# First attention of a 16-sequence block on one core: gate features stacked into 96 rows, product with values by quarters, tiles closed a pass later

## The chip, the cores and the metric

The kernel runs on one core of one Trainium2 chip. The metric is the device time of one execution, in microseconds (us); lower is better. The engines are PE (TensorE), DVE (VectorE), ACT (ScalarE), POOL (GpSimd) and SP (SyncE, which here only issues DMAs).

## What is computed

X is 16 sequences of 128 tokens of 256 numbers. It goes through an attention over a context with a relational gate, a feed-forward net, a second attention and a mixture of experts. The change lies in the first attention alone:

```python
q = (queries @ Wq.T + bq).reshape(b, nq, H, D_K).transpose(0, 2, 1, 3)      # H = 16, D_K = D_V = 64
...
g = relu(einsum('bnmd,hd->bhnm', emb, Wg) + bg[None, :, None, None])        # emb: sin and cos of 100 * log box differences
a = einsum('bhqd,bhkd->bhqk', q, k) / sqrt(D_K)
mn = softmax(log(clip(g, 1e-06, None)) + a, axis=-1)
out = einsum('bhqk,bhkd->bqhd', mn, v).reshape(b, nq, H * D_V)
return out @ Wo.T + bo
```

emb has, for each pair of tokens (n, m) of a sequence, the sine and cosine of two frequencies of four differences: of the centres in x and y, relative to a size, and of the logarithms of width and height. The kernel computes the softmax numerator as max(g, 1e-6) * exp(a), so the gate is a factor. Width and height differences split into products of terms of n and of m and come from tables; centre differences don't, and are worked out for each pair.

## The kernel before

A tile is one sequence; there are 16, b = 0 to 15. Each engine runs a program of its own, written out by hand, and they meet at semaphores; the order on an engine is the order of the code. The programs are software-pipelined: in one pass (`iteration(b)`) every engine does a different part for tile b-1, b, b+1 and b+2. Products that need accuracy use pairs of fp16 numbers, a high part (a copy, made by ACT) and a low part (the rest, by a subtraction on POOL), and three matmuls for high x high, high x low and low x high.

One pass of the engines, in words, with the line numbers of the profile:

- **PE**: scores of tile b in four groups (lines 1762, 1769), among them the gates of tile b, one for each of four PSUM banks (`gate`: a table product of `Lst`, line 1784, and the feature product, line 1788, of `F16s` with the block-diagonal weights `We16`), row scores for the maximum (1747), project_qk (1719) of tile b+1, then `pv` of tile b-1 (1807: probabilities with values, four quarters f of 4 heads), project_v (1730), turn_o (1821), turn_xn (1696) and project_o (1827) of tile b-1.
- **VectorE**: `norm` (868), row maxima (879) and take_qk (899) in two pairs each, take_pv (888 the reciprocal of the denominators, 891 the division) of tile b-1, the floor of the centre differences ahead of the logarithm (852), take_v (908), turns (857), xn_low (873), `residual` of tile b-1 (914 writes `otmp`, 917 adds it to X), fractions (861, 863), distance (845), and, when the exponentials of tile b are there, `probs` (928: clip, times exponential) and the statistics of the new X (1017).
- **ScalarE**: exponentials (1424), sine (1393) and the high part of the features (1397), high parts of the probabilities (1450), of q and k (1437) and of v (1442), logarithm (1386), take_o (1408).
- **POOL**: low parts of the probabilities (565, four of them), of the features (560), of q and k (551, four), of v (556, two), of the context (521), and two DMAs that turn a half of one expert's weights to fp16 for a later stage (574, 578).
- **SP**: for each tile a load of context (343), of its gate tables (`load_tables`, 396, three transfers of 68 KB, after the gate of two tiles before), the store (368) and load (374) of expert halves; at b = 8 the second half of the gate tables is stored (386, 387). At the end the weights of the feed-forward net (421 to 424), on which `ternary_scale` (961 on, VectorE) waits.

The features stand with one of 128 rows for each of x or y, sine or cosine, two frequencies and 16 tokens n; columns are the 8 blocks of n and the tokens m. The gate's six matmuls of 256 columns (16 heads x 16 tokens n) use all 128 rows.

## Time and profile before

| | |
|---|---|
| median of three runs | 1148.08 us (1142.33 to 1149.12) |
| profiled execution | 1143.62 us |
| its span, first to last instruction | 1141.6 us |
| busy, of the span | PE 949.0 (83%), VectorE 817.9 (72%), ScalarE 684.2 (60%), POOL 710.1 (62%) |
| mean granted clock of TensorE | 0.929 |

The first attention takes the stretch from about 24 to 480 us, its middle tiles that from 100 to 401. Everything behind 480 us is not touched by the change. The rows that follow below are of this one profiled execution, on a scale that begins with its first instruction.

### The profile page before, as it was taken

What the parts mean: (1) busy time and instruction counts of PE and PEld (TensorE: products, weight loads), DVE (VectorE), ACT (ScalarE), POOL (GpSimd) and SP (SyncE); (2) the same over time, 40 slices, a digit from 0 to 9 for tenths busy, and PEclk for the clock granted to TensorE, in tenths of its full rate; (3) what the DMA queues carried; (4) which work ended last, traced back from release to release, by engine and by line L of the source; (5) the groups of instructions that cost most, each with busy time, mean ns of one, the idle gap of its engine ahead of it and who ended that gap; (6) DMA issues with size and microseconds to landing.
All of it is one profiled execution on the core that took longest, in us unless ns stands there. A gap on an engine that the chain in (4) does not pass through costs nothing.

```text
span 1141.6 us, 32938 instructions
## 1 busy us (share of the span) xinstructions
PE 949.0 (83%) x12178; PEld 777.1 (68%) x12178; DVE 817.9 (72%) x1957; ACT 684.2 (60%) x1342; POOL 710.1 (62%) x811
## 2 busy tenths in 40 slices
PE   0448999999999985589876569982899999999995
PEld 0336777777777764455544458861899999999995
DVE  3997888788877876677877689956566666666663
ACT  2457888888888883066543468854354454545452
POOL 2988888875777653035453279965466666666662
PEclk9889999999999997689988789985899999999998
DMA  9277776787767656411000100003553225832251
GB/s 280 76 188 150 135 150 153 157 175 171 146 154 159 137 109 167 143 51 41 1 1 1 40 2 21 21 21 100 165 152 103 33 40 168 268 91 32 32 143 14
DMA packets 52117, 119.65 MB, mean 105 GB/s; under 512 B 7616, under 2 KB 30144, under 8 KB 51632
## 3 DMA queue, kind: packets, MB, share of 16 engines
q0 software_dynamic: 14144, 35.48, 21.6%
q1 hardware_dynamic: 35520, 80.71, 21.1%
q10 hardware_dynamic: 2352, 2.10, 0.6%
q8 instruction: 66, 1.08, 0.4%
q14 instruction: 35, 0.29, 0.1%
HBM read 212.54 MB, written 37.85 MB: 219 GB/s over the span
## 4 chain that ended last, share of the span: by engine, by line
PE 53%; DVE 14%; POOL 11%; ACT 9%; DMA 7%; issue 5%; SPq 0%; ACTq 0%; POOLq 0%; DVEq 0%
PE bank L2168 17%; PE bank L2182 8%; POOL PT L565 6%; PE bank L1827 5%; PE bank L1730 3%; PE bank L1929 3%; DVE nmx L1209 2%; PE bank L1968 2%; PE bank L1807 2%; ACT EX L1424 2%; PE bank L1941 2%; PE bank L1769 2%; ACT L1393 1%; PE bank L1762 1%; DMA gates<-in_g_ffn 1%
## 5 line engine op out<-in xcount | busy, mean ns | idle before, releaser
L1664 ACT ACTIVATE yg<-bank,bms 128x128 f32<-128x128 f32 x312 | 106.9, 363 | 113.2 <-PE bank L2168 103.3
L1327 DVE TENSOR_TENSOR hm<-hf,hm 128x256 f16<-128x256 f32 x156 | 66.7, 427 | 90.8 <-ACT hm L1671 87.0
L1322 DVE SCALAR_TENSOR_TENSOR hf<-bank,bms,yg 128x128 f32<-128x128 f32 x312 | 98.8, 347 | 32.1 <-ACT yg L1664 29.4
L2168 PE MATMUL bank<-xT,wm_even 128*128 128x128 f16 x1920 | 116.2, 221 | 1.9 <-DVE xT L1334 1.0
L709 POOL DMA_INDIRECT out_x<-ys,sidx x39 | 62.7, 1608 | 83.2 <-DVE ys L1341 83.2
L2168 PEld LDWEIGHTS bank<-xT,wm_even 128*128 128x128 f16 x1920 | 111.5, 99 | 3.5 <-DVE xT L1334 1.4
L2168 PE MATMUL bank<-xT,wm_odd 128*128 128x128 f16 x1824 | 109.9, 220 | 2.0 <-DMA wm_odd<-expert_weights 2.0
L2168 PEld LDWEIGHTS bank<-xT,wm_odd 128*128 128x128 f16 x1824 | 105.5, 99 | 3.1 <-issue 2.2
L1671 ACT ACTIVATE hm<-hf 128x256 f16<-128x256 f32 x156 | 64.7, 415 | 63.9 <-DVE hf L1322 62.8
L565 POOL TENSOR_TENSOR PT<-PT 128x512 f16<-128x512 f32 x64 | 72.3, 1157 | 41.7 <-ACT PT L1450 41.6
L551 POOL TENSOR_TENSOR q<-qt,q 128x512 f16<-128x512 f32 x64 | 79.9, 1276 | 1.0 <-ACT q L1437 0.9
L670 POOL TENSOR_TENSOR P<-P 128x512 f16<-128x512 f32 x64 | 72.9, 1171 | 11.5 <-ACT P L1620 11.5
L635 POOL TENSOR_TENSOR h<-h 128x512 f16<-128x512 f32 x32 | 37.3, 1166 | 50.1 <-ACT h L1524 24.5
L702 POOL DMA_INDIRECT xin<-expert_tokens,gidx x39 | 44.5, 1141 | 30.8 <-POOL b2r L724 26.3
L1827 PE MATMUL bank<-WoT,OT 128*128 128x256 f32 x256 | 59.5, 386 | 1.9 <-ACT OT L1408 1.9
L2182 PE MATMUL bank<-wm_even,hm 128*128 128x256 f16 x480 | 57.4, 278 | 2.3 <-DVE hm L1327 2.3
L1437 ACT ACTIVATE q<-qt 128x512 f16<-128x512 f32 x64 | 38.9, 626 | 34.0 <-DVE qt L899 34.0
L1807 PE MATMUL bank<-vv,PT 128*128 128x65 f16 x768 | 33.9, 200 | 28.0 <-POOL PT L565 17.8
L1827 PEld LDWEIGHTS bank<-WoT,OT 128*128 128x128 f32 x256 | 47.3, 190 | 11.7 <-ACT OT L1408 5.9
L578 POOL DMA_DIRECT2D wsp<-in_wcat x16 | 19.6, 1222 | 56.3 <-ACT wsp L1414 56.0
L719 POOL TENSOR_SCALAR gts<-xin,etf 128x1 f32<-128x1 f32 x78 | 53.4, 911 | 0.7 <-DMA xin<-expert_tokens,gidx 0.6
L1788 PE MATMUL bank<-We,F16s 128*128 128x256 f16 x384 | 53.7, 277 | 0.0
(309 smaller groups left out, 2660.2 us busy)
## 6 DMA issues: line engine op xcount, KB each, us to landing
wm_even<-expert_weights SPq DMA_DIRECT2D x60, 1024.0 KB
wm_odd<-expert_weights SPq DMA_DIRECT2D x57, 1024.0 KB
expert_weights<-in_wcat POOLq DMA_DIRECT2D x16, 768.0 KB, 7.8
wsp<-expert_weights SPq DMA_DIRECT2D x16, 768.0 KB, 4.4
wsp<-in_wcat POOLq DMA_DIRECT2D x16, 768.0 KB, 10.6
expert_weights<-wsp SPq DMA_DIRECT2D x16, 768.0 KB, 3.3
Lst<-gate_tables SPq DMA_DIRECT2D x48, 68.0 KB, 5.8
gate_tables<-Lw SPq DMA_DIRECT2D x6, 512.0 KB, 4.6
```

The costliest lines, as they stand in the source:

```text
L551: nc.gpsimd.tensor_tensor(q16[:, par, w, 1, HS * g:HS * g + HS, :], qt[:, r, :, :], hi, ALU.subtract).then_inc(s_ql, 1)
L565: nc.gpsimd.tensor_tensor(PT16[:, 1, HS * g:HS * g + HS, :], PT[:, HS * g:HS * g + HS, :], PT16[:, 0, HS * g:HS * g + HS, :], ALU.subtract ...
L670: nc.gpsimd.tensor_tensor(P116[:, b % 2, 1, HS * g:HS * g + HS, :], P1[:, b % 2, HS * g:HS * g + HS, :], P116[:, b % 2, 0, HS * g:HS * g + ...
L709: nc.gpsimd.indirect_dma_start(out=a["out"], out_offset=bass.IndirectOffsetOnAxis(ap=sidx[:, t:t + 1], axis=0), in_=ys[:, t % 2, :], in_of ...
L1322: v.scalar_tensor_tensor(hf[:, (c // 2) % 2, c % 2, :], bank[c % 4][:, MT:2 * MT], bms[:, par, FC + c:FC + c + 1], yg[:, c % 4, :], ALU.ad ...
L1327: v.tensor_tensor(hm16[:, par, 1, c - 1:c + 1, :], hf[:, q % 2, :, :], hm16[:, par, 0, c - 1:c + 1, :], ALU.subtract).then_inc(m_hl, 1)
L1664: s.activation(yg[:, c % 4, :], bank[c % 4][:, 0:MT], ACT.Gelu, bias=bms[:, par, c:c + 1]).then_inc(m_g, 1)
L1671: s.activation(hm16[:, par, 0, 2 * q:2 * q + 2, :], hf[:, q % 2, :, :], ACT.Copy).then_inc(m_hh, 1)
L1807: ins = t.matmul(bank[6 + f % 2][:, i * (DK + 1):(i + 1) * (DK + 1)], PT16[:, pp, sl, :], vv16[:, par, vp, sl, :], start=(n == 0), stop=(n ...
L1827: ins = t.matmul(bank[7][:, 0:D], OT[:, ch, :], WoT[:, ch, :], start=(ch == 0), stop=(ch == CH - 1))
L2168: ins = t.matmul(bank[c % 4][:, w * MT:(w + 1) * MT], wm16[par][:, wp, col:col + P], xT16[:, par, xp * KD + kk, :], start=(n == 0), stop=( ...
L2182: ins = t.matmul(bank[5 + par][:, 0:D], hm16[:, par, xp, c, :], wm16[par][:, wp, col:col + D], start=(n == 0), stop=(n == 3 * FC - 1))
```

## The change

**Features in 96 rows.** `F16s`, high and low part, is no longer double-buffered, and its rows are ordered so that 32 neighbouring rows hold a quarter q of each block's 16 tokens n. SP copies it with 12 DMAs of 32 rows x 2 KB (64 KB each) into `Fst`, of 96 rows: for each quarter the high part twice and the low part once. The weights are stacked to match (high, low, high), so that one matmul of 96 rows and 64 columns (16 heads x 4 tokens) does for a quarter what three of 128 rows did for 256 columns: 8 matmuls take the place of 6 for each gate. The gate waits for the 12 DMAs of its tile, the writers of `F16s` for those of the tile before. The box coordinates come ready-laid in two loads in place of four broadcasts.

**Product with values.** `pv` waits for the low parts of the probabilities quarter by quarter, no longer for all four at its front.

**Closing a tile.** residual and statistics move from the pass after the tile's to the one after that, between the first take_qk pair and the second pair of row maxima (`close_tile(b - 2)`); `norm` moves from the front of a pass to just ahead of the `probs` of the pass before. In the last pass `ternary_scale` is no longer ahead of `probs` but behind the close of tile 14.

**Table wait.** The wait for the second tables' stores stands behind the stacks of tile 7.

```diff
+QN = 4
+QR = 2 * QN * 4
+FR = 3 * QR
+STK = 16 * 3 * (NN // QN)
...
-        F16s = sb("F16s", [P, 2, 2, NJ * N], F16, l0)
+        F16s = sb("F16s", [P, 2, NJ * N], F16, l0)
+        Fst = sb("Fst", [P, NN // QN, NJ * N], F16, l0)
...
-        We = sb("We", [P, H * NN], F32, l0)
-        We16 = sb("We16", [P, 2, H * NN], F16, l0)
+        We = sb("We", [P, H * QN], F32, l0)
+        We16 = sb("We16", [P, H * QN], F16, l0)
...
-                sp.wait_ge(s_ts, 96 * g + 96)
+                if g == 0:
+                    sp.wait_ge(s_ts, 96)
...
+            def stack_high(b):
+
+                sp.wait_ge(s_fhi, b + 1)
+                if b:
+                    sp.wait_ge(s_gf, 4 * b)
+                for q in range(NN // QN):
+                    for k in range(2):
+                        sp.dma_start(Fst[k * QR:k * QR + QR, q, :], F16s[q * QR:q * QR + QR, 0, :]).then_inc(s_fst, 16)
+
+            def stack_low(b):
+
+                sp.wait_ge(s_flo, b + 1)
+                for q in range(NN // QN):
+                    sp.dma_start(Fst[2 * QR:3 * QR, q, :], F16s[q * QR:q * QR + QR, 1, :]).then_inc(s_fst, 16)
+
             for par in range(2):
                 next_ctx(par, par)
+            stack_high(0)
             store_tables(0)
             for par in range(2):
                 load_tables(par)
+            stack_low(0)
             for par in range(2):
                 load_half(0, par, True)
-            for i in range(1, B // 2 - 1):
-                for par in range(2):
-                    next_ctx(i * 2 + par, par)
-                    if i * 2 + par == NJ:
-                        store_tables(1)
-                    load_tables(i * 2 + par)
-                    store_half(i - 1, par)
-                    load_half(i, par)
-            for par in range(2):
-                load_tables(B - 2 + par)
-                store_half(E - 2, par)
-                load_half(E - 1, par)
-
+            for b in range(2, B):
+                par = b % 2
+                if b < B - 2:
+                    next_ctx(b, par)
+                if b == NJ:
+                    store_tables(1)
+                    stack_high(b - 1)
+                    stack_low(b - 1)
+                    sp.wait_ge(s_ts, 192)
+                load_tables(b)
+                if b != NJ:
+                    stack_high(b - 1)
+                    stack_low(b - 1)
+                store_half(b // 2 - 1, par)
+                load_half(b // 2, par)
+
+            stack_high(B - 1)
+            stack_low(B - 1)
...
             def feature_low(n, par):
                 gp.wait_ge(s_fhi, n + 1)
-                nc.gpsimd.tensor_tensor(F16s[:, par, 1, :], fs, F16s[:, par, 0, :], ALU.subtract).then_inc(s_flo, 1)
+                if n:
+                    gp.wait_ge(s_fst, STK * n)
+                nc.gpsimd.tensor_tensor(F16s[:, 1, :], fs, F16s[:, 0, :], ALU.subtract).then_inc(s_flo, 1)
...
             def residual(c):
                 dv.wait_ge(s_op, c + 1)
-                v.tensor_tensor(otmp[:, :], bank[7][:, 0:D], bo[:, :], ALU.add).then_inc(s_opt, 1)
-                dv.wait_ge(s_opt, c + 1)
+                step(v.tensor_tensor(otmp[:, :], bank[7][:, 0:D], bo[:, :], ALU.add))
                 xb = X[:, bass.ds(c, 1), :]
                 v.scalar_tensor_tensor(xb, otmp[:, :].unsqueeze(1), tg[:, 0:1], xb, ALU.mult, ALU.add).then_inc(s_xu, 1)
...
             def iteration(b, par, has_c, has_q, has_x, first=False):
-                if has_x:
+                if not has_c:
                     norm(b + 2, b + 2)
                 row_max(b, (0, 1))
                 if has_q:
                     take_qk(b + 1, (0, 1))
+                if b > 1:
+                    close_tile(b - 2)
                 row_max(b, (2, 3))
                 if has_q:
                     take_qk(b + 1, (2, 3))
@@ -1002,19 +1033,19 @@
                     feature_turns(b + 1, 1 - par)
                 if has_x:
                     xn_low(b + 2, par)
-                if has_c:
-                    residual(b - 1)
-                    dv.wait_ge(s_xu, b)
                 if has_q:
                     feature_fractions(b + 1, 1 - par)
-                if not has_q:
-                    ternary_scale()
                 if has_x:
                     dv.wait_ge(s_fa, 3 * b + 3)
                     feature_distance(b + 2, par)
+                if b + 3 < B:
+                    norm(b + 3, b + 3)
                 probs(b, not has_c)
-                if has_c:
-                    v.bn_stats(bst[:, bass.ds(b - 1, 1), :].rearrange("p o c -> p (o c)"), X[:, bass.ds(b - 1, 1), :].rearrange("p o d -> p (o d)"))
+
+            def close_tile(c):
+                residual(c)
+                dv.wait_ge(s_xu, c + 1)
+                return v.bn_stats(bst[:, c, :], X[:, c, :])
 
             iteration(0, 0, False, True, True)
             iteration(1, 1, True, True, True, True)
@@ -1023,12 +1054,11 @@
                     iteration(i * 2 + 2 + par, par, True, True, True)
             iteration(B - 2, 0, True, True, False)
             iteration(B - 1, 1, True, False, False)
+            close_tile(B - 2)
...
+            ternary_scale()
             ternary_hidden()
             take_pv(B - 1)
-            residual(B - 1)
-
-            dv.wait_ge(s_xu, B)
-            v.bn_stats(bst[:, B - 1, :], X[:, B - 1, :]).then_inc(s_bs, 1)
+            close_tile(B - 1).then_inc(s_bs, 1)
...
-                if first > 1:
-                    ac.wait_ge(s_gf, 4 * n - 4)
-                s.activation(F16s[:, par, 0, :], fs, ACT.Copy).then_inc(s_fhi, 1)
+                if n:
+                    ac.wait_ge(s_fst, STK * n)
+                s.activation(F16s[:, 0, :], fs, ACT.Copy).then_inc(s_fhi, 1)
...
             def gate(b, par, g, first, has_q):
                 if g == 0:
-                    pe.wait_ge(s_flo, b + 1)
+                    pe.wait_ge(s_fst, STK * (b + 1))
                     pe.wait_ge(s_tl[par], (b - par) * 24 + 48)
 
                 n = b + 1 if has_q else b
@@ -1784,21 +1814,22 @@
                 t.matmul(bk[:, :], Lst[0:3 * SLOTS, par, GL:], Lst[0:3 * SLOTS, par, g * 512:g * 512 + 512], start=True, stop=True)
                 for jj in range(2):
                     j = 2 * g + jj
-                    for n, (wp, fp) in enumerate(PAIRS):
-                        ins = t.matmul(bk[:, jj * 256:(jj + 1) * 256], F16s[:, par, fp, j * N:(j + 1) * N], We16[:, wp, :], start=False,
-                                       stop=(n == 2), skip_group_check=True)
+                    part = bk[:, jj * 256:(jj + 1) * 256].rearrange("p (h q i) -> p q h i", h=H, q=NN // QN)
+                    for q in range(NN // QN):
+                        ins = t.matmul(part[:, q, :, :], Fst[0:FR, q, j * N:(j + 1) * N], We16[0:FR, :], start=False, stop=True,
+                                       skip_group_check=True)
                 ins.then_inc(s_gf, 1)
 
             def pv(c, par, first):
-                pe.wait_ge(s_pl, 4 * c + 4)
                 pe.wait_ge(s_vl, 2 * c + 2)
                 for f in range(4):
+                    pe.wait_ge(s_pl, 4 * c + f + 1)
                     if f == 0:
                         pe.wait_ge(s_xh, xl_of(c))
                         pe.wait_ge(s_xl, xl_of(c))
                     elif f == 1:
                         if not first:
-                            pe.wait_ge(s_opt, c)
+                            pe.wait_ge(s_xu, c)
                     else:
                         pe.wait_ge(s_oe, 4 * c + f - 1)
...
-            pe.wait_ge(s_opt, B)
+            pe.wait_ge(s_xu, B)
...
-    We = np.zeros((2, 2, 2, NN, H, NN), np.float32)
+    We = np.zeros((3, 2, 2, 2, QN, H, QN), np.float32)
     for xy in range(2):
         for sc in range(2):
             for fr in range(2):
-                for nn in range(NN):
-                    We[xy, sc, fr, nn, :, nn] = feat(sc, xy, fr)
-    a["We"] = We.reshape(P, H * NN)
+                for i in range(QN):
+                    We[:, xy, sc, fr, i, :, i] = feat(sc, xy, fr)
+    a["We"] = We.reshape(FR, H * QN)
```

VectorE, one middle pass from the end of `probs` to the first reciprocal; `nmx` are the row maxima, `qt` take_qk, `rden` the reciprocal, `otmp` and `X` the residual. Before:

```order
L1017 BN_STATS bst<-X 128x6
L868 TENSOR_SCALAR xn<-X,mv,rstd 128x256 [waits xn_turned]
L879 TENSOR_REDUCE nmx<-bank 128x4 [waits row_scores] x2
L899 SCALAR_TENSOR_TENSOR qt<-bank,bqk 128x512 [waits qk_low,qkv_full] x2
L879 TENSOR_REDUCE nmx<-bank 128x4 [waits row_scores] x2
L899 SCALAR_TENSOR_TENSOR qt<-bank,bqk 128x512 [waits qk_low,qkv_full] x2
L888 RECIPROCAL rden<-bank 128x4 [waits pv_taken,pv_full]
```

After (line 909 is the row maximum, 929 take_qk, 944 and 946 the residual, 1048 the statistics, 918 the reciprocal):

```order
L909 TENSOR_REDUCE nmx<-bank 128x4 [waits row_scores] x2
L929 SCALAR_TENSOR_TENSOR qt<-bank,bqk 128x512 [waits qk_low,qkv_full] x2
L944 TENSOR_TENSOR otmp<-bank,bo 128x256 [waits proj_full]
L946 SCALAR_TENSOR_TENSOR X<-otmp,tg,X 128x256 [waits prefix_vector]
L1048 BN_STATS bst<-X 128x6 [waits x_updated]
L909 TENSOR_REDUCE nmx<-bank 128x4 [waits row_scores] x2
L929 SCALAR_TENSOR_TENSOR qt<-bank,bqk 128x512 [waits qk_low,qkv_full] x2
L918 RECIPROCAL rden<-bank 128x4 [waits pv_taken,pv_full]
```

The three instructions that close a tile now stand between the two pairs ahead of the division, where statistics and norm had stood in front of the first pair.

SP, one middle tile, an odd one, from its context load to its expert half. Before:

```order
L343 DMA ctxf<-in_ctxT 128x2x128 [waits ctx_low,ctx_high]
L396 DMA Lst<-gate_tables 16x2176 [waits gate_full]
L396 DMA Lst<-gate_tables 16x2176 x2
L368 DMA expert_weights<-wsp 128x3072 [waits half_expert_low_odd]
L374 DMA wsp<-expert_weights 128x3072 [waits half_expert_stored_odd,half_expert_high_odd]
```

After, `Fst<-F16s` being the stack, high parts (411) and low parts (417):

```order
L349 DMA ctxf<-in_ctxT 128x2x128 [waits ctx_low,ctx_high]
L402 DMA Lst<-gate_tables 16x2176 [waits gate_full]
L402 DMA Lst<-gate_tables 16x2176 x2
L411 DMA Fst<-F16s 32x1024 [waits gate_full,gate_high]
L411 DMA Fst<-F16s 32x1024 x7
L417 DMA Fst<-F16s 32x1024 [waits gate_low]
L417 DMA Fst<-F16s 32x1024 x3
L373 DMA expert_weights<-wsp 128x3072 [waits half_expert_low_odd]
L379 DMA wsp<-expert_weights 128x3072 [waits half_expert_stored_odd,half_expert_high_odd]
```

Twelve transfers stand between the table loads and the store of an expert half, the last four behind a wait for POOL's low part of the features (`gate_low`).

PE, one middle pass, from the second half of project_qk to the first project_v. Before:

```order
L1719 MATMUL bank<-ctx,wqkv 128x128 [waits probs_ready]
L1719 MATMUL bank<-ctx,wqkv 128x128 x23
L1807 MATMUL bank<-vv,PT 128x65 [waits xn_high,xn_low,values_low,probs_low]
L1807 MATMUL bank<-vv,PT 128x65 x11
L1807 MATMUL bank<-vv,PT 128x65 [waits proj_taken]
L1807 MATMUL bank<-vv,PT 128x65 x11
L1807 MATMUL bank<-vv,PT 128x65 [waits pv_taken]
L1807 MATMUL bank<-vv,PT 128x65 x11
L1807 MATMUL bank<-vv,PT 128x65 [waits pv_taken]
L1807 MATMUL bank<-vv,PT 128x65 x11
L1730 MATMUL bank<-wqkv,ctx 128x512 [waits qkv_taken]
```

After:

```order
L1749 MATMUL bank<-ctx,wqkv 128x128 [waits probs_ready]
L1749 MATMUL bank<-ctx,wqkv 128x128 x23
L1838 MATMUL bank<-vv,PT 128x65 [waits xn_high,xn_low,probs_low,values_low]
L1838 MATMUL bank<-vv,PT 128x65 x11
L1838 MATMUL bank<-vv,PT 128x65 [waits x_updated,probs_low]
L1838 MATMUL bank<-vv,PT 128x65 x11
L1838 MATMUL bank<-vv,PT 128x65 [waits pv_taken,probs_low]
L1838 MATMUL bank<-vv,PT 128x65 x11
L1838 MATMUL bank<-vv,PT 128x65 [waits pv_taken,probs_low]
L1838 MATMUL bank<-vv,PT 128x65 x11
L1760 MATMUL bank<-wqkv,ctx 128x512 [waits qkv_taken]
```

Each quarter now has its own wait for a low part of the probabilities, and the second one waits for the update of X (`x_updated`) where it had waited for `proj_taken`.

## Rows read from the trace of the kernel before

**Rows 1.** Stage table: length, busy us by engine (x instructions), clock, DMA.

```profile
100.00:401.00 301.00, 286.96 (x3658) 217.79 (x3658) 240.36 (x548) 258.38 (x368) 227.37 (x209) 1.00 0.74 154
```

**Rows 2.** Chain of waits, tiles 7 to 8: start us, us, what ran.

```profile
233.91 1.28 ACT L1393
...
257.58 1.28 ACT L1393
```

**Rows 3.** VectorE in order of time, tile 8: start us, us, instruction.

```profile
260.31 0.42 DVE L1017 BATCH_NORM_STATS2 bst<-X 128x6 f32<-128x256 f32 x1
...
260.95 1.29 DVE L879 TENSOR_REDUCE nmx<-bank 128x4 f16<-128x512 f32 x2
...
265.85 0.69 DVE L899 SCALAR_TENSOR_TENSOR qt<-bank,bqk 128x512 f32<-128x512 f32 x1 [0.62 <-PE bank L1719]
266.77 0.18 DVE L888 RECIPROCAL rden<-bank 128x4 f32<-128x4 f32 x1 [0.23 <-PE bank L1807]
...
269.16 0.74 DVE L852 TENSOR_SCALAR fu<-fu 128x1024 f32<-128x1024 f32 x1
...
276.76 0.49 DVE L917 SCALAR_TENSOR_TENSOR X<-otmp,tg,X 128x256 f32<-128x256 f32 x1
```

**Rows 4.** ScalarE in order of time, the logarithm in tile 8.

```profile
269.94 1.06 ACT L1386 ACTIVATE fu<-fu 128x1024 f32<-128x1024 f32 x1 [0.48 <-DVE fu L852]
```

**Rows 5.** POOL in order of time, tile 8, then tile 14.

```profile
261.63 4.51 POOL L565 TENSOR_TENSOR PT<-PT 128x512 f16<-128x512 f32 x4 [4.17 <-ACT PT L1450]
266.11 2.13 POOL L560 TENSOR_TENSOR F16s<-fks,F16s 128x1024 f16<-128x1024 f32 x1
268.20 1.15 POOL L551 TENSOR_TENSOR q<-qt,q 128x512 f16<-128x512 f32 x1
269.31 1.61 POOL L551 TENSOR_TENSOR q<-qt,q 128x512 f16<-128x512 f32 x1
...
431.35 2.12 POOL L560 TENSOR_TENSOR F16s<-fks,F16s 128x1024 f16<-128x1024 f32 x1
```

**Rows 6.** All engines in order of time near 451 us.

```profile
451.32 0.41 DVE L973 TENSOR_SCALAR fu<-wqkv,thr 128x256 f32<-128x256 f32 x1
...
451.51 2.39 POOL L565 TENSOR_TENSOR PT<-PT 128x512 f16<-128x512 f32 x2 [6.07 <-ACT PT L1450]
451.64 1.25 DVE L972 TENSOR_SCALAR wqkv<-wqkv,thr 128x256 f32<-128x256 f32 x1
```

**Rows 7.** PE in order of time: gate, half a pv, gate, pv(14).

```profile
235.08 0.83 PE L1788 MATMUL bank<-We,F16s 128*128 128x256 f16 x6
...
243.87 1.09 PE L1807 MATMUL bank<-vv,PT 128*128 128x65 f16 x24 [0.36 <-DVE O L891]
...
277.32 0.38 PE L1784 MATMUL bank<-Lst 48*128 48x512 f16 x1
...
431.44 3.08 PE L1807 MATMUL bank<-vv,PT 128*128 128x65 f16 x48 [3.70 <-POOL PT L565]
```

**Rows 8.** SyncE's DMA issues in order of time, tile 8.

```profile
259.61 1.32 SPq L396 DMA_DIRECT2D Lst<-gate_tables  x3
```

**Rows 9.** Line 396 alone, 250 to 290 us: issue to landing.

```profile
DMA to landing us min/median/max: 5.1/5.7/6.6
```

**Rows 10.** All engines in order of time, tile 1.

```profile
100.49 2.14 POOL L560 TENSOR_TENSOR F16s<-fks,F16s 128x1024 f16<-128x1024 f32 x1
...
103.56 0.73 DVE L852 TENSOR_SCALAR fu<-fu 128x1024 f32<-128x1024 f32 x1
```

**Rows 11.** Chain of waits, end of the stage.

```profile
433.80 8.71 DMA fgate<-in_fgate
```

**Rows 12.** VectorE in order of time, end of the stage.

```profile
442.61 2.29 DVE L961 TENSOR_REDUCE thr<-wqkv 128x8 f32<-128x2048 f32 x1 [0.97 <-DMA fgate<-in_fgate]
...
448.02 2.74 DVE L928 SCALAR_TENSOR_TENSOR PT<-bank,EX 128x256 f32<-128x256 f32 x8
...
461.96 0.18 DVE L888 RECIPROCAL rden<-bank 128x4 f32<-128x4 f32 x1
```

26 lines of the change are left out of this document (14 added, 12 removed).

## The prediction

> **What bounds the kernel now.** Read first the stage table: between 100 and 401 us the thirteen middle tiles of the first attention run, PE is busy 287 of 301 us, DVE 240, ACT 258, POOL 227, and the granted clock is 1.00, the 2.4 GHz level [rows 1]. All four engines are so full that the share of no one decides; the reader is to look for a chain. The chain of waits gives it [rows 2]: the last exponential of a tile ends (I call this time zero: 257.56 us for tile 8), ACT loads its sine table and takes the sine of the next tile's features, turns the probabilities of this tile into fp16 (line 1450), POOL makes four low parts of them in a row (line 565, 4.51 us of them from 261.63 [rows 5]), PE multiplies with the values, and after VectorE's division come project_v, turn_o, project_o, the scores and the next exponential. From the table load at 233.91 to the next at 257.58 that is 23.67 us for the tile [rows 2].
>
> A second path ties up with it. In the rows of VectorE, tile 8, the first division starts at 266.77 (9.21 after zero) and the floor of the features (line 852) at 269.16 (11.60), ending at 269.90 (12.34) [rows 3]. ScalarE's logarithm comes right at the floor's end, and behind the logarithm on ScalarE stand the high part of the values and take_o, which feeds project_o [rows 4]. POOL ends its fourth probability low near 266.2, then makes the low feature part (2.13 us) and the first low part of q from 268.20 to 269.35 (11.79), and the second takes 1.61 us in place of 1.15 [rows 5]. That second is prolonged because the floor ran inside it: floor and POOL don't run at the same time. The same is clear where VectorE has nothing else: line 973 takes 0.41 us with POOL idle, and line 972, no longer by itself, takes 1.25 us once POOL's low parts have begun at 451.51 [rows 6]. So an instruction of VectorE that reads and writes SBUF can wait for the running one of POOL, and then holds up POOL's next. From these rows: it ends some 0.3 to 0.55 us after POOL's does. The floor was issued at 11.60, 0.19 us ahead of the end of the first q low; it ends 0.55 after that end wherever in this q low it was issued.
>
> **Part 1, the gate from 96 rows.** Before, one gate is a table matmul and six of 256 columns, 0.83 us [rows 7]. After, it is the table matmul and eight of 64 columns. The nearest row has 65 columns: 24 in 1.09 us, 0.045 each [rows 7], eight make 0.36, so a gate gets about 0.4 us shorter. The chain holds no gate row in a middle tile [rows 2]: PE waits for an exponential behind it. Gain on the path: 0, and the cover is that exponential. What it costs is on SP: 12 issues for each tile. Issues take 0.44 each (three in 1.32) [rows 8]. Eight go out behind the table loads, about 3.4 to 6.9 after zero, and four behind the low feature part, which ends at 10.68 and, moved as below, at 10.9: so the last is issued at 12.7. These are 64 KB; the 68 KB of a table's third land after 5.7 us in the median, 6.6 at most [rows 9], so all is stacked by 18.4, at the latest by 19.3. The gate of the next tile wants it at 277.32, which is 19.76 [rows 7]: 0.5 us of cover are left in the worst case. Moved 768 KB a tile across SBUF, on engines busy 0.74 of the time [rows 1]; expert halves behind them on SP start some 3 us later, and are not needed before the next tile. The added waits of ScalarE (feature copy) and POOL (feature low) ask for the stack of the tile before, 7 us old by then: 0. On this transfer the Trainium skill ("DMA: Bandwidth & Descriptors", the section on the fixed cost) has about 2 us for a transfer; by that the stack would stand at about 15 and this cover would be 4 us and more. The rows under load decide here, and the sum is the same by both.
>
> **Part 2, pv a quarter at a time.** In a middle tile PE has project_qk in front of pv: VectorE's last take_qk waits 0.62 us for it and starts at 8.29 [rows 3]. The first quarter of pv can't start much before that, and VectorE is not free for its division before 9.46 (below): 0. In tile 1 VectorE comes to the division sooner than pv does, and there it can start about 1.1 us sooner; the floor (before: 103.56 to 104.29) then falls into the low feature part that ends at 102.63, and ends 0.55 after it, at 103.2 [rows 10]: **-1.1 us**, once. In the tile before last, PE is idle ahead of pv (3.70 us idle, then 3.08 us of pv after 431.44) [rows 7]: three quarters of these can go under POOL's work, 2.3 us. This brings the last exponential forward, but the stage's end hangs on another thing (part 4).
>
> **Part 3, VectorE closes a tile a pass later.** Bn_stats and norm leave the front of a pass (260.31 to 260.95, 0.64 us) [rows 3], so the first row_max and take_qk start 0.64 sooner, and take_qk is done at 5.15. Now otmp, X and bn_stats come, 0.46 + 0.52 + 0.34 = 1.32 us by pitch. But X reads and writes SBUF, and POOL is in its probability lows (261.63 on, 1.12 apart: the second from 5.19 to 6.34) [rows 5]. Before, X ran at 276.76 while POOL was idle [rows 3]. By the rule of [rows 6] it ends at about 6.7 in place of 6.1, bn_stats at 7.06, the second row_max and take_qk run until 9.46, and the third probability low, held up by X, is 0.23 late, and all of POOL behind it. So the first division is at 9.46 (before 9.21), the four divisions bring the floor's issue to 11.85, and the first q low ends at 12.02 (11.79 + 0.23): the floor still gets in with 0.17 us to spare, and ends at 12.57, **+0.23 us** for each tile, logarithm, take_o and project_o with it. For thirteen tiles **+3.0**. What was taken out of the second half of the pass (otmp and X, 0.98 us) gives slack only: probs waits for the exponential, not for VectorE. Bounds: if X isn't held, VectorE reaches the divisions at 8.9, PE's pv sets them, and the tile costs 0; if the floor could then come free of POOL altogether, the logarithm could start 0.48 us sooner, when its table is loaded [rows 4]: -0.48 a tile, -6.2 in all. Upper end: rival A.
>
> **Part 4, the end.** The FFN weights are issued on SP after POOL's low feature part, and fgate, the last of five issues, goes out at 433.80 and lands 8.71 later, at 442.51 [rows 11]; ternary_scale waits for it and starts at 442.61 [rows 12]. After, the stack of tile 15 stands ahead of them on SP, and its last four issues wait for the low feature part of that tile, which ends at 433.47 [rows 5] and now, in the clock of before, at 433.7. Four issues of 0.44 take SP to 435.5, the five of the weights (2.9 from the first's start to the last's) to 438.4, and fgate lands at 447.1, 4.6 later. By then the probabilities of tile 15 are made (they don't wait for the scale any more). Then come 5.4 us of ternary_scale (442.61 to 448.0 before), the 16 instructions of lines 972 and 973 at their free pitch of 0.32 us (5.2 us: some took 1.25 before, since POOL's last low parts ran beside them [rows 6]; these now run beside the scale), and 2.3 us of line 975: the division at 460.0 to 460.9. Before it was at 461.96 [rows 12]. I take **-1.5 us**. The start, with other sizes of loads and the first stack ahead of the table stores, is within 1 us of 0.
>
> **Sum** against the profiled execution (1143.62, its span 1141.6): -1.1 + 3.0 - 1.5 = +0.4, so 1144. The three runs have their median at 1148.08, 4.5 above it; the forecast is carried to it: **1148.5 us**.
>
> **Rivals.** *A, slower: the floor misses the first q low.* If VectorE comes at 12.02 or later (the margin is 0.17 us, less than I know the times of X and the third low), the second q low starts ahead of it and the floor ends at 1.12 + 0.55 after that: about 1.1 us later a tile than in my forecast. 13 x 1.1 = 14.3, with the rest 1162.8. For it: a margin of 0.17. Against it: floor and q low are moved by the same cause. It decides from a shift of 0.17 us.
> *B, X isn't held up or POOL isn't late.* Then terms are -1.1 - 1.5 = -2.6: 1145.5, down to 1139.3 with -0.48 a tile. For it: otmp runs ahead of X, so X may come just ahead of the second low's start (5.61 against 5.19, needs 0.42). The Trainium skill ("SBUF — State Buffer", "SBUF: two separate sides") has the port pair of the two engines locked by whichever instruction starts first, if VectorE's has two inputs in SBUF or a two-port mode; X has two inputs, and the trace agrees that such ones are held. Beyond it by 1%: only if also the end gives all of the 2.4 us and each tile 0.48 and more.
> *C, the stack lands late.* If landings take 1 us more than the 6.6 at most, the gate of the second exponential group waits and the period gets 0.5 to 1 us longer: +7 to +13, to 1155 to 1161. Transfers of POOL fill the engines in the first 9 us of a tile, and the stack comes among them.
>
> **Chances.** Forecast 0.42, A 0.24, B 0.26, C 0.08. One per cent (11.5 us) is about what a measurement of this kernel can tell from no change. Slower by over 1%: A and a part of C, 0.27. Faster by over 1%: a quarter of B, 0.07. Range: from B's lower end, 1139, to A, 1164.
>
> **What would show it.** In the changed profile: the first division at 9.4 to 9.5 after the last exponential, X (line 946) of about 1.1 us in place of 0.49, the third line 595 longer, floor of 0.74 ending 12.5 to 12.6, a second q low of 1.6. If line 882 shows near 1.2 us or more and ends at 13.7, it is A. If the gate's first matmul waits for a DMA, it is C. Line 990 (the first of ternary_scale) starting right after the landing of fgate, some 4 us after the probabilities of tile 15 could begin, shows part 4. I would be wrong most of all if ScalarE's order left the logarithm on another release than the floor.

## The result

| | before | changed |
|---|---|---|
| median of five runs | 1146.15 us | 1154.82 us (1152.69 to 1155.08) |
| profiled execution | 1143.62, span 1141.6 | 1155.08, span 1153.2 |
| mean granted clock | 0.929 | 0.915 |

The changed kernel takes 1.0088 times as long as the one before, with a 95% interval of 1.0061 to 1.0116. It is slower, by 8.7 us in the medians and 11.6 in the profiled spans.

Where it went is read from marks that every trace has: the sine table load of ScalarE, which follows a tile's last exponential, and the first matmul of the feed-forward net behind the attention. In the chain of waits of the kernel before that matmul is at 479.17, in the changed kernel at 495.31:

```profile
479.17 1.22 PE bank L1884 x2
```

```profile
495.31 5.06 PE bank L1915 x11
```

So the attention is 16.1 us longer, and the rest of the program, which the change does not touch, 4.5 us shorter (657.9 in place of 662.4). The 16.1 are: 5.8 up to the first sine (95.99 in place of 90.22), 7.1 over the fourteen tiles from there (339.73 in place of 332.63), 3.3 behind the last of them.

**Middle tiles.** The stage table of the changed kernel, against that of [rows 1]: PE is 25 us less busy, VectorE 22 us more, DMA 0.86 in place of 0.74, and the clock is 0.98.

```profile
100.00:401.00 301.00, 261.88 (x3727) 207.34 (x3725) 262.79 (x533) 249.54 (x359) 228.25 (x208) 0.98 0.86 183
```

VectorE and POOL in the same tile as [rows 3, 5]; its zero is at 268.06.

```profile
273.65 1.04 DVE L946 SCALAR_TENSOR_TENSOR X<-otmp,tg,X 128x256 f32<-128x256 f32 x1
...
277.46 0.17 DVE L918 RECIPROCAL rden<-bank 128x4 f32<-128x4 f32 x1
...
279.90 0.68 DVE L882 TENSOR_SCALAR fu<-fu 128x1024 f32<-128x1024 f32 x1
```

```profile
272.14 4.69 POOL L595 TENSOR_TENSOR PT<-PT 128x512 f16<-128x512 f32 x4 [4.17 <-ACT PT L1480]
...
279.99 1.62 POOL L579 TENSOR_TENSOR q<-qt,q 128x512 f16<-128x512 f32 x1
```

The reader is to see X at 1.04 in place of 0.49, the four low parts at 4.69 in place of 4.51, the first division 9.40 after zero (9.21 before), the floor issued at 11.84 (11.60), inside the first low part of q, and the second low part of q at 1.62. The late X also stands in the chain of waits of the changed kernel, here in one of the last tiles, and the row maxima, take_qk and the divisions follow it there:

```profile
417.13 0.34 DVE otmp L944
417.49 1.06 DVE X L946
```

Tile k is here, as tile 8 in the prediction, the stretch from its predecessor's sine load to its own. The loads that end tiles 7 to 11 of the changed kernel are 23.8 apart, but for the last pair, 24.9:

```profile
268.08 1.28 ACT L1423 ACT_TABLE_LOAD   x1
...
291.87 1.28 ACT L1423 ACT_TABLE_LOAD   x1
...
315.67 1.28 ACT L1423 ACT_TABLE_LOAD   x1
...
339.45 1.28 ACT L1423 ACT_TABLE_LOAD   x1
...
364.35 1.28 ACT L1423 ACT_TABLE_LOAD   x1
```

In this long tile, 11, the third division waits for PE a quarter of a microsecond more, the floor is issued 12.08 after the table load, when POOL has gone over to the second low part of q (350.25 to 351.40 was the first), and takes 1.54:

```profile
350.42 0.18 DVE L918 RECIPROCAL rden<-bank 128x4 f32<-128x4 f32 x1 [0.41 <-PE bank L1838]
...
351.53 1.54 DVE L882 TENSOR_SCALAR fu<-fu 128x1024 f32<-128x1024 f32 x1
```

**Start.** SyncE's issues:

```profile
60.66 5.06 SPq L411 DMA_DIRECT2D Fst<-F16s  x8
65.82 0.53 SPq L391 DMA_DIRECT2D gate_tables<-Lw  x1
...
79.24 3.01 SPq L402 DMA_DIRECT2D Lst<-gate_tables  x6
82.30 2.42 SPq L417 DMA_DIRECT2D Fst<-F16s  x4
84.76 1.08 SPq L379 DMA_DIRECT2D wsp<-expert_weights  x2
```

The stack of tile 0 takes SP 5.06 us (0.63 an issue; a table load takes 0.44 [rows 8]). The table stores go out behind it, and the last of them takes 10.07 us to land:

```profile
69.16 10.07 DMA gate_tables<-R
```

In the kernel before it went out at 65.44, and the table loads that wait for it started 3.0 us later, at 68.47. What lies beside it here are two loads of 768 KB that POOL issues from 68.54 on; before, the stores were down when these went out, at 68.92. So the table loads start at 79.24, and the first load of an expert half, for which ScalarE and with it the first exponential wait, goes out at 84.76. Before it went out at 77.16. It lands 1.4 us faster (4.6 in place of 6.0), which leaves about 6 us of the delay.

**End.** PE's two last project_o are 5.56 and 6.36 us long. Before, each took 3.72; the first of the rows is that of tile 14 before, the others are those of the changed kernel:

```profile
436.94 3.72 PE L1827 MATMUL bank<-WoT,OT 128*128 128x256 f32 x16 [0.69 <-ACT OT L1408]
```

```profile
447.87 5.56 PE L1858 MATMUL bank<-WoT,OT 128*128 128x256 f32 x16 [0.69 <-ACT OT L1438]
...
480.40 6.36 PE L1858 MATMUL bank<-WoT,OT 128*128 128x256 f32 x16 [0.69 <-ACT OT L1438]
```

### The profile page after: what moved, and what is told of

Its sections match the earlier page's. It is cut to its first block, busy times and chain, and to the rows that moved or that the text cites. A ratio compares the mean times of both kernels' runs of the same rounds, so it can differ in the third digit from the quotient of the medians.

```text
span 1153.2 us, 33447 instructions
## 1 busy us (share of the span) xinstructions
PE 928.9 (81%) x12306; PEld 771.3 (67%) x12306; DVE 845.8 (73%) x1957; ACT 687.4 (60%) x1342; POOL 713.7 (62%) x811
## 4 chain that ended last, share of the span: by engine, by line
PE 56%; DVE 26%; ACT 6%; issue 5%; DMA 4%; SPq 1%; POOL 1%; ACTq 0%; POOLq 0%; DVEq 0%
PE bank L2199 18%; PE bank L2213 9%; PE bank L1858 5%; DVE qt L929 3%; DVE PT L957 3%; PE bank L1760 3%; PE bank L1960 3%; DVE nmx L909 2%; PE bank L1799 2%; DVE nmx L1239 2%; PE bank L1999 2%; PE bank L1972 2%; ACT EX L1454 2%; PE bank L1792 1%; PE bank L1838 1%
## 5 line engine op out<-in xcount | busy, mean ns | idle before, releaser
L1357 DVE TENSOR_TENSOR hm<-hf,hm 128x256 f16<-128x256 f32 x156 | 69.8, 448 | 82.1 <-ACT hm L1701 82.1
L595 POOL TENSOR_TENSOR PT<-PT 128x512 f16<-128x512 f32 x64 | 74.7, 1195 | 40.9 <-ACT PT L1480 40.8
L957 DVE SCALAR_TENSOR_TENSOR PT<-bank,EX 128x256 f32<-128x256 f32 x128 | 43.8, 414 | 34.3 <-PE bank L1819 25.4
L1858 PE MATMUL bank<-WoT,OT 128*128 128x256 f32 x256 | 63.9, 406 | 1.8 <-ACT OT L1438 1.8
L1838 PEld LDWEIGHTS bank<-vv,PT 128*128 128x128 f16 x768 | 29.5, 102 | 48.3 <-issue 44.9
L732 POOL DMA_INDIRECT xin<-expert_tokens,gidx x39 | 42.1, 1080 | 30.8 <-POOL b2r L754 26.3
L1858 PEld LDWEIGHTS bank<-WoT,OT 128*128 128x128 f32 x256 | 50.5, 203 | 12.9 <-ACT OT L1438 5.8
L749 POOL TENSOR_SCALAR gts<-xin,etf 128x1 f32<-128x1 f32 x78 | 56.1, 1084 | 0.7 <-DMA xin<-expert_tokens,gidx 0.7
```

The lines of the kernel that those rows point to most:

```text
L595: nc.gpsimd.tensor_tensor(PT16[:, 1, HS * g:HS * g + HS, :], PT[:, HS * g:HS * g + HS, :], PT16[:, 0, HS * g:HS * g + HS, :], ALU.subtract ...
L957: v.scalar_tensor_tensor(PT[:, :, j * NN:(j + 1) * NN], bank[2 + g][:, jj * 256:(jj + 1) * 256].rearrange("p (h n) -> p h n", h=H), 1e-6 * ...
L1357: v.tensor_tensor(hm16[:, par, 1, c - 1:c + 1, :], hf[:, q % 2, :, :], hm16[:, par, 0, c - 1:c + 1, :], ALU.subtract).then_inc(m_hl, 1)
L1838: ins = t.matmul(bank[6 + f % 2][:, i * (DK + 1):(i + 1) * (DK + 1)], PT16[:, pp, sl, :], vv16[:, par, vp, sl, :], start=(n == 0), stop=(n ...
L1858: ins = t.matmul(bank[7][:, 0:D], OT[:, ch, :], WoT[:, ch, :], start=(ch == 0), stop=(ch == CH - 1))
```

## The experiments

All times are of traces, except the ratio, which is that of the timed runs to those of the kernel before on the same chip, with its 95% interval. "Tiles" is the sum of the fourteen periods, "behind" the time from the sine load of tile 14 to the first matmul of the feed-forward net, "rest" that from there to the end.

| kernel | first sine | tiles | behind | rest | ratio |
|---|---|---|---|---|---|
| before | 90.2 | 332.6 | 56.3 | 662.4 | |
| changed | 96.0 | 339.7 | 59.6 | 657.9 | 1.0088 (1.0061 to 1.0116) |
| e1_close_back | 95.4 | 332.5 | 63.0 | 667.7 | 1.0118 (1.0088 to 1.0149) |
| e2_start_order | 91.6 | 337.4 | 59.7 | 664.6 | 1.0086 (1.0055 to 1.0117) |
| e3_close_front | 95.6 | 347.0 | 57.7 | 666.3 | 1.0198 (1.0171 to 1.0224) |
| e4_close_only | 90.3 | 341.6 | 59.1 | 665.2 | 1.0073 (1.0050 to 1.0096) |
| e5_start_close_nofloor | 90.8 | 333.6 | 63.3 | 661.1 | 1.0023 (0.9993 to 1.0053) |
| e6_before_nofloor | 89.7 | 334.8 | 59.6 | 661.2 | 1.0018 (0.9997 to 1.0039) |
| e7_after_nofloor | 94.9 | 337.2 | 57.1 | 662.3 | 1.0068 (1.0044 to 1.0093) |
| e8_quarters_only | 90.0 | 334.0 | 59.9 | 658.1 | 1.0021 (1.0002 to 1.0040) |
| e9_quarters_nofloor | 89.2 | 330.4 | 59.5 | 656.4 | 0.9962 (0.9945 to 0.9979) |
| e10_after_whole_tail | 94.9 | 338.6 | 59.7 | 656.4 | 1.0092 (1.0061 to 1.0123) |
| e11_start_loads_first | 98.5 | 334.6 | 59.6 | 658.1 | one run |
| e12_after_whole_pv | 95.2 | 337.3 | 59.6 | 658.2 | 1.0079 (1.0054 to 1.0104) |

The rest is the same code in all of them and lies between 656.4 and 667.7 (last section). That hides or doubles what a kernel gains in the attention, so the columns before it are what tells theories apart.

Each row is one trace, and its columns move from trace to trace too. The changed kernel and e10 are the same program up to the product of tile 14 with the values; yet the first sine is at 95.99 in the one and at 94.86 in the other, tile 1 takes 26.48 and 24.23 us, and the long tiles are 2, 3 and 11 in the one and 8, 11, 12 and 13 in the other. So a difference of about 1 us at the start, or of 2 us in tile 1, tells nothing of an edit. The sum of tiles 2 to 14 is steadier: 307.1 to 307.3 in the three kernels that have the floor and the old place of the close (before, e1, e8), and 311.9 to 314.8 in the six with the floor and the close between the two pairs (changed, e2, e4, e10, e11, e12).

**e1_close_back: the third part undone.** Against the changed kernel:

```diff
+                if has_x:
                     norm(b + 2, b + 2)
                 row_max(b, (0, 1))
...
-                if b > 1:
-                    close_tile(b - 2)
...
+                if has_c:
+                    residual(b - 1)
```

> The changed kernel with its third part undone: residual, statistics, norm and ternary_scale stand where they stood before; the stacked features, the quarter waits and the order on SP stay. Theory 1 (what the middle tiles lose comes from X and the floor beside POOL): the middle period is 23.6 us again in place of 23.8, no floor takes over 0.8 us, tiles 1 to 3 lose their 1.1 to 1.5 us as far as a missed floor made them; 4 to 6 us faster than the changed kernel, and still 5 to 6 us late at the first sine. Theory 2 (the shorter gate leaves PE idle and its clock falls): tiles 1 to 3 stay at 25 us and the gain is under 3 us.

Theory 1 holds for the attention. The tiles are 332.5, tiles 2 to 14 each 23.59 to 23.67, as before the change (332.6), and the clock of the middle stage is 1.00. So the 6.0 us that tiles 2 to 14 lost are the third part's; the 1.1 us of tile 1 are within what that tile moves by itself. The row of the floor, in tile 9, says why the first two parts gave nothing:

```profile
294.99 0.17 DVE L918 RECIPROCAL rden<-bank 128x4 f32<-128x4 f32 x1
...
297.44 1.22 DVE L882 TENSOR_SCALAR fu<-fu 128x1024 f32<-128x1024 f32 x1
```

In this row the first division is 8.64 after the sine table load that opens the tile (before 9.20), the floor is issued at 11.09 (before 11.58), and takes 1.22 in place of 0.74, so that it ends at 12.3 as before. The gain of 0.5 us is eaten by POOL. The time behind the tiles is 3.4 us worse than the changed kernel's: ternary_scale stands ahead of probs again and waits 6.17 us for a weight that now lands at 452.4. With this and a long rest (667.7) its ratio is no better than the changed kernel's, 1.0118 against 1.0088 with intervals that overlap, though its attention ends 4.3 us sooner. The 4 to 6 us that theory 1 had for the total did not show.

**e2_start_order: SP's order at the start.**

```diff
-            stack_high(0)
             store_tables(0)
             for par in range(2):
                 load_tables(par)
+            stack_high(0)
+            load_half(0, 0, True)
             stack_low(0)
-            for par in range(2):
-                load_half(0, par, True)
+            load_half(0, 1, True)
```

> The changed kernel with another order on SP at the start: tables are stored and loaded first, then the high stack of tile 0, then the first expert half is loaded, then the low stack, then the second half. Theory 1 (the 5.8 us at the start are SP's queue: eight stack issues ahead of the table stores and four ahead of the expert load that the first exponential waits for): the first sine table load at 90 to 92 us in place of 95.99, 4 to 6 us faster. Theory 2 (the first gate waits for the stack itself): it stays at 94 us or later.

The first sine is at 91.56, 4.4 us sooner. So the order on SP's queue makes most of the start's loss: the last table store is out at 64.29, ahead of POOL's loads, and the table loads follow 3.0 us later as in the kernel before. The load goes out at 76.2, but lands after 8.76 us and not 6.0. Theory 2 is not borne out. The attention ends 6.6 us sooner (488.7); the total gains nothing, since the rest is 6.7 us longer than in the changed kernel.

**e3_close_front: the close where POOL is idle.**

```diff
+                if b > 1:
+                    close_tile(b - 2)
                 row_max(b, (0, 1))
                 if has_q:
                     take_qk(b + 1, (0, 1))
-                if b > 1:
-                    close_tile(b - 2)
```

> The changed kernel with the close of a tile at the very front of a pass, ahead of the first row maximum, where POOL is idle. Theory 1 (X is held by POOL's low part of the probabilities): X takes 0.49 in place of 1.05 us, the first division starts at 8.8 to 9.0 after the last exponential in place of 9.40, the third low part is not prolonged, and the middle period is 23.6 or less in place of 23.8: 2 to 6 us faster. Theory 2 (it is the place ahead of the division that costs, three instructions more whatever POOL does): division at 9.4 and 23.8 us stay.

X takes 0.48 and the low parts 4.50, so X had been held by POOL. But the division came at 9.29, not 8.8 to 9.0, and the period is 24.7: both theories missed. Rows of one tile, whose table load is at 294.35:

```profile
297.53 0.48 DVE L946 SCALAR_TENSOR_TENSOR X<-otmp,tg,X 128x256 f32<-128x256 f32 x1
...
303.64 0.17 DVE L918 RECIPROCAL rden<-bank 128x4 f32<-128x4 f32 x1
...
306.10 1.68 DVE L882 TENSOR_SCALAR fu<-fu 128x1024 f32<-128x1024 f32 x1
```

```profile
298.40 4.50 POOL L595 TENSOR_TENSOR PT<-PT 128x512 f16<-128x512 f32 x4 [4.18 <-ACT PT L1480]
...
304.95 4.95 POOL L579 TENSOR_TENSOR q<-qt,q 128x512 f16<-128x512 f32 x4
```

POOL's first low part of q starts at 304.95 and ends at 306.10 (1.15 later); the floor is issued at that same 306.10 and takes 1.68. Here rival A of the prediction is in every tile, by hundredths, and costs 0.93 a tile (24.72 against 23.79). In the changed kernel the held X had also prolonged POOL's low parts (4.69), so that the first low part of q ended 11.93 after zero there and ends at 11.75 here; that had let the floor get in. A free X did not bring the division to 8.9 either, as the prediction's lower bound had it: VectorE's last take_qk now waits 0.38 us for project_qk.

**e4_close_only: the third part on the kernel before.** The edit is the diff's, on `iteration` and the end of VectorE's program alone.

> The kernel before with the third part alone: tiles closed a pass later, norm ahead of probs, ternary_scale behind the last pass; gate, quarter waits and SP as before. Theory 1: the first sine at 90.2 us as before, middle period 23.8 (X 1.05 us) and a missed floor in some tiles, together 3 to 6 us slower over the stage than before. Theory 2 (the middle tiles lose by the stack's transfers or by the clock): the period stays at 23.6.

Period 23.87, and four irregular tiles (4, 9 and 10 with 24.99, 26.16 and 24.90, and tile 1 with 26.82): 8.9 us over the tiles, more than the 3 to 6 of theory 1; without tile 1 it is 7.5, against 6.0 in the changed kernel. So the third part costs about the same, or more, without stack and quarter waits. But it does so in another way in most tiles. X takes 0.48 there and not the 1.05 that I expected: VectorE's second take_qk waits 0.55 us for project_qk, which the longer gates delay, so X comes 0.64 later and falls between two of POOL's parts. The division is still at 9.46. A held X is therefore not the only way in which three more instructions ahead of the division make it late. In tiles 9 and 10 X is held, for 1.51 us, and the division comes at 10.5.

**e5, e6, e7: without the floor.** The clip of the centre differences is taken out from between the divisions and the logarithm, with the same result but for rounding:

```diff
-                    feature_floor(b + 1, 1 - par)
...
-                s.activation(fu[:, par, :], fu[:, par, :], ACT.Ln).then_inc(s_fa, 1)
+                s.activation(fu[:, par, :], fu[:, par, :], ACT.Ln, bias=cst[:, 7:8], scale=cst[:, 6:7]).then_inc(s_fa, 1)
...
-                v.tensor_scalar(fu[:, par, :], fu[:, par, :], cst[:, 0:1], cst[:, 1:2], ALU.mult, ALU.add).then_inc(s_fv, 1)
+                v.tensor_scalar(fu[:, par, :], fu[:, par, :], cst[:, 0:1], cst[:, 1:2], ALU.mult, ALU.max).then_inc(s_fv, 1)
```

> The changed kernel with the third part undone, SP's order at the start as in the second run, and without the floor: the clip of the centre differences at 1e-3 is no instruction of VectorE between the divisions and the logarithm any more; the logarithm takes a scale that carries the quarter turn, and the clip is the maximum that turns (line 887) takes behind it. Same numbers but for rounding. Theory 1 (stacked gate and quarter waits let VectorE come 0.2 to 0.6 us sooner to the divisions, and the floor, held to the end of POOL's first low part of q, eats that): the middle period falls from 23.6 to about 23.1, the logarithm starts at the end of its table load; with the start at 91.5 the stage ends 10 us or more ahead of the changed kernel. Theory 2 (another release stands right behind the floor): 23.5 or more.

> The kernel before without the floor (the same rewriting), nothing of the change in it. Theory 1: project_o there waits for PE's own path (divisions, project_v, turn_o) as much as for take_o, so without the gate's and the quarters' share the period falls by no more than 0.1 to 0.2 us from 23.61. Theory 2 (the floor alone carries all of the gain): 23.1, as in the run above.

> The changed kernel without the floor and nothing else altered. Theory 1 (the irregular tiles are those in which the floor misses POOL's first low part of q): tiles 3 and 11 have the period of the others, all from 23.5 to 23.8, and X stays at 1.05 us; stage shorter by 4 to 6 us, the 5.8 us at the start stay. Theory 2: tiles 1 to 3 stay at 25 us, because the clock and not the floor makes them.

In e5 the last tiles have 23.08, against 23.60 in e1: the floor had eaten half a microsecond of the first two parts. But its stage ends 7.7 us ahead of the changed kernel's and not the 10 of theory 1, for one thing because tile 7 took 28.77 us. Its chain of waits:

```profile
247.54 0.59 SPq L417
...
249.44 7.70 DMA Fst<-F16s
...
257.18 0.60 PE bank L1813
```

That is rival C: in the pass in which SP also stores the second tables, the last stack transfer lands after 7.70 us and the gate waits for it, and PE then runs at the lower clock (0.50) for some 8 us. In the same pass of the changed kernel the last stack transfers landed after 2.0 to 2.4 us. In e6 the tiles from 9 on keep 23.6, as theory 1 had it, but tiles 2 to 7 get 24.1, which neither had. There the probabilities wait for the distances (line 845) on VectorE, which are late without the floor. In e7 tile 11 is regular (23.82), where it takes 24.9 in all four kernels that have the third part, the floor and the quarter waits of tile 11 (changed, e2, e10, e11), so its floor had made it long. Tiles 2 and 3 stay at 25.0 without a floor (tile 1 takes 24.95), so theirs had another cause, and the granted clock is at the lower level in both; and the period stays at 23.81, so the late division costs the tile its 0.2 us by PE's way too.

**e8_quarters_only.**

```diff
-                pe.wait_ge(s_pl, 4 * c + 4)
                 pe.wait_ge(s_vl, 2 * c + 2)
                 for f in range(4):
+                    pe.wait_ge(s_pl, 4 * c + f + 1)
```

> The kernel before with the quarter waits of pv alone. Theory 1: middle period 23.6 as before (the floor is held by POOL wherever it is issued in the first low part of q), tile 1 shorter by about 1 us, and in the last passes pv(14) ends 2 us sooner but project_o that follows runs at the lower clock (over 5 us in place of 3.72), so that the stage's end gains less than 1 us. Theory 2 (the clock falls there because of the stacked gate): project_o(14) stays at 3.72 and the last exponential comes 2 us sooner.

Period 23.6 as forecast, but tile 1 takes 26.82 and not 24.3: the gates ahead of it, at the lower clock, take 1.46 us up to the one at 93.05; before, the last such gate is at 89.44 and that at 91.24 takes 0.83. So project_qk and the division are late. These gates run ahead of the first product with values (100.60 in the kernel before), the first place at which the edit can act, so the edit doesn't make them slow. What tile 1 takes moves with the clock from 22.6 to 26.8 over all kernels. Project_o(14) takes 5.82 us, as theory 1 had it.

**e10_after_whole_tail.**

```diff
+                whole = c >= B - 2
+                if whole:
+                    pe.wait_ge(s_pl, 4 * c + 4)
                 pe.wait_ge(s_vl, 2 * c + 2)
                 for f in range(4):
-                    pe.wait_ge(s_pl, 4 * c + f + 1)
+                    if not whole:
+                        pe.wait_ge(s_pl, 4 * c + f + 1)
```

> The changed kernel, but the products of tiles 14 and 15 with the values wait for all four low parts again. Theory 1 (the quarter waits leave PE working in pieces between POOL's low parts, its clock falls and project_o pays it back): project_o(14) takes 3.72 us again in place of 5.56, and from the sine load of tile 14 to the last exponential it stays 22.7 us. Theory 2 (the stacked gate or the moved close makes the slow clock): project_o(14) stays over 5 us and the last exponential comes 2 us later.

```profile
442.23 3.08 PE L1842 MATMUL bank<-vv,PT 128*128 128x65 f16 x48 [4.01 <-POOL PT L595]
...
447.59 3.72 PE L1862 MATMUL bank<-WoT,OT 128*128 128x256 f32 x16 [0.74 <-ACT OT L1438]
...
478.21 6.44 PE L1862 MATMUL bank<-WoT,OT 128*128 128x256 f32 x16 [0.69 <-ACT OT L1438]
```

3.72 us again, as in e12. With e8 this shows that the quarter waits make project_o(14) slow: pv ends 2 us sooner with them, PE has worked in pieces before, and project_o gives the 2 us back at the lower clock. Project_o(15) stays at 6.44. It takes 6.07 in e6, which has nothing of the change, and 3.72 in e3 and e7, which have nearly all of it: the 2.7 us there are not the change's.

**e11_start_loads_first.** As e2, with both loads of expert halves ahead of the whole stack of tile 0.

> The changed kernel with both first loads of expert halves ahead of the stack on SP at the start. In the second run the load went out at 76.2 as in the kernel before, but took 8.8 us in place of 6.0. Theory 1 (the stack's transfers share the load's way, and the load is on the chain to the first exponential): with the stack behind it the load lands after 6 us, and then the first gate waits for the stack, so that the first sine is at 91 to 93 us all the same. Theory 2 (something else in the changed kernel lengthens the load): it takes 8 us or more again.

The load lands after 6.2 us or less, so theory 1 is right in that. But the first sine is at 98.53, later than in the changed kernel, because the chain now goes through the stack: its last transfer is issued at 88.65 and lands 5.30 us later, and the first gate waits for it. In each of the three orders tried something behind the twelve issues waits. The range of 91 to 93 was too good.

**e12_after_whole_pv: the second part undone.** The reverse of e8's edit, on the changed kernel.

> The changed kernel without its second part: every product with values waits for all four low parts, as before. In the changed kernel PE runs the first two quarters early and then idles 2.1 us until VectorE's divisions come; in the tiles of 25 us its clock falls to the 1.2 GHz level just behind that gap, the third quarter comes late and the floor misses POOL's first low part of q. Theory 1 (that gap, made by quarter waits together with late divisions, is the cause): no gap over 1.3 us ahead of the divisions, granted clock 1.00 in tiles 2 and 3, all tiles from 2 on at 23.8 to 23.9 us; 3 to 5 us shorter over the stage than the changed kernel. Theory 2 (the floor misses by its 0.2 us of margin alone, or the stacked gate lowers the clock): some tiles of about 25 us remain.

Theory 1 falls. Two tiles, 2 and 4, of 25.08 and 24.95 us remain, with two missed floors. In tile 2 PE's clock is at the lower level for most of the 4 us behind the first division, 0.57 in the mean (the figures are length, busy us of PE, weight loads, VectorE, ScalarE and POOL, then clock, DMA share and GB/s):

```profile
120.50:130.50 10.00, 7.96 (x149) 7.02 (x145) 9.81 (x21) 7.86 (x12) 9.14 (x10) 1.00 1.02 175
130.50:134.50 4.00, 3.86 (x32) 2.28 (x33) 3.28 (x8) 2.71 (x4) 4.00 (x4) 0.57 0.34 77
```

Tile 2 of the changed kernel for comparison:

```profile
122.45:133.50 11.05, 8.61 (x171) 7.76 (x168) 10.62 (x25) 8.91 (x14) 10.18 (x11) 1.00 0.91 140
133.50:136.50 3.00, 3.00 (x19) 1.86 (x16) 2.18 (x5) 2.43 (x3) 3.00 (x3) 0.62 0.31 74
```

Of the kernels in this study, all with the close between the two pairs have such tiles (changed, e2, e4, e7, e10, e11, e12); e3, and those with the close in its old place, have none, but for the tiles of e5 around the late stack. So it is the third part as it stands, with or without quarter waits or stack. What PE does differently in the long tiles and in their neighbours, whose rows are alike up to there, I can't see. Other long tiles, as tile 11 of the changed kernel and tile 4 of e4 and e12, have the clock at 1.00 and a floor that came 0.2 us late, and why it came late in these is open as well.

**e9_quarters_nofloor: what beats both.** The kernel before without the floor, and with quarter waits in all tiles but the last two; e10's edit and e5's, no others.

> The kernel before without the floor and with the quarter waits of pv in tiles 0 to 13 (the last two products wait for all four low parts, as before). No stacked gate, no moved close. Theory 1 (two paths tie, ScalarE's behind the floor and PE's behind the divisions, so that only both together shorten a tile): the period from tile 8 on falls to 23.2 to 23.4 us where each of the two alone left 23.6, project_o(14) takes 3.72 us, and the stage ends 2 to 4 us ahead of the kernel before. Theory 2 (the shorter gate was what shortened the tiles to 23.08): 23.6 stays.

```profile
279.62 1.28 ACT L1391 ACT_TABLE_LOAD   x1
...
302.94 1.28 ACT L1391 ACT_TABLE_LOAD   x1
```

23.32 us a tile from tile 8 on, where each of the two edits alone left 23.60. Theory 1 holds for the period and for project_o(14), but the stage ends 0.2 us ahead of the kernel before and not 2 to 4. The kernel takes 0.9962 of the time before, a gain of 4.3 us with an interval from 2.4 to 6.3. In the profiled executions its attention ends at 479.0, where that of the kernel before ends at 479.2 with a project_o(15) of 3.72 us; this kernel's takes 6.44. Against e6 (484.1) and e8 (483.8), whose project_o(15) is as slow, it is 5 us sooner. How much of the 4.3 us comes from the attention and how much from the rest is not settled.

## Why the prediction was right where it was, and wrong in its steps

The time of 1154.8 lies in the range, and the change is within 1%; forecast was +0.4 us, measured +8.7. That it lies there is in part luck. The attention alone lost 16.1 us, of which the sum had 3.0 in the middle tiles and -2.6 elsewhere, and a rest that was 4.5 us shorter hid a part. By the steps:

- **Part 3, middle tiles: right in mechanism and size.** X held by POOL was forecast at 1.1 and measured at 1.04 to 1.11, the first division at 9.46 (measured 9.40), the floor's issue at 11.85 (11.84), a regular tile at +0.23 (+0.18). e1 shows that it is this part. Two things were incomplete. e7 shows the same period without a floor, so PE's way is as long, and ScalarE's is not the only one. And e3 and e4 have late divisions (9.29 and 9.46) with a free X, so the bound of 8.9 for a free X was wrong: project_qk had been taken to be in time.
- **The margin of 0.17 us: decided in some tiles.** I had the floor get in or miss in all tiles alike. Of the thirteen from tile 2 on it gets in in eleven and misses in two, tile 3 and tile 11. Tile 11 is 1.1 us longer than its neighbours, the 1.1 of rival A. Tile 3, at the lower clock too, is 1.35 longer, and tile 2, at the lower clock with the floor in time, 1.2. Together these make 4 us that the sum had not.
- **Part 1, no gain on the path: right**, but not for the reason given. The shorter gate does bring VectorE to the divisions sooner (8.64 in e1, against 8.88 in e8 and 9.20 before); the floor takes it back. The cover for the stack was put at 0.5 us in the worst case, from landings of 5.7 to 6.6. The last four transfers of a stack, on which it rests, landed after 1.9 to 3.8 us in the middle tiles, so it was over 2 us in tile 7 and over 3 in tile 9, nearer to the other estimate of the prediction. In e5 it failed all the same, with one landing of 7.70.
- **Part 1 at the start: the step that failed most.** I wrote "within 1 us of 0". It is +5.8. A stack issue takes 0.63 us and not 0.44, eight of them stand ahead of the table stores, the last store then takes 10.07 us to land in place of about 3, beside POOL's loads, and the load of the first expert half, which the first exponential waits for, stands behind everything. That the store is slow because of POOL's loads fits e2 and was not tested by itself. I had worked the queue for a middle tile and for the end, and not for the start.
- **Part 2 in tile 1: not borne out** (forecast -1.1, measured +1.1), but the +1.1 is no effect of this part that the runs show. The time of that tile follows from when PE's clock rises, which the sum left out, and moved by 2.3 us between the changed kernel and e10, the same program there. That VectorE reaches the floor sooner was not seen in the changed kernel.
- **Part 2 and 4 at the end: -1.5 forecast, +0.6 measured** up to the last division (39.69 after the table load in place of 39.11), and 2.7 more in project_o(15), which is not the change's. The last exponential was to come 2.3 us sooner and came at the same place, as project_o(14) ran at the lower clock. So ternary_scale (462.41) waited for VectorE's own work and not for fgate: for the probabilities of tile 15 and the close of tile 14 (1.3 us), which the part of the sum on the end had put at nothing.

The 16.1 us of these two traces are then, but for rounding: start 5.8, tile 1 1.1, the ten regular tiles 1.8, tiles 2, 3 and 11 4.2 (the lower clock in the first two, a missed floor in the last two), end 0.6, project_o(15) 2.7. The first two can be 1 to 2 us off by the spread that e10 shows. The 4.5 us less in the rest are no effect of any edit that I could name.

## What to carry to other kernels

Where an instruction of VectorE on the chain must come between two of POOL's, work out when it is issued against the end of POOL's, because a gain of half a microsecond ahead of it can come out as nothing, and a loss of a few hundredths as nearly a whole instruction. Taking that instruction off the chain paid only together with a shorter way on the other path (e9, 0.3 us a tile); alone (e6), as the quarter waits alone (e8), it gave nothing. Transfers added to one queue are to be followed through every place in which the program issues them, the start above all, where something waits behind each. And a stage's own marks in the trace tell more than the total when later stages have rhythms of their own.
